# TensorE's program written out instead of looped, in a three-stage fp32 kernel (RWKV mixing, experts, output)

## The reference, cut to what matters

```python
xn = layernorm(x)                                   # x: (8, 512, 512) fp32
# attention branch (RWKV)
xk, xv, xr, xg = (xn + (prev(xn) - xn) * tm for tm in (tm_k, tm_v, tm_r, tm_g))
k, v, r, g = xk @ Wk.T, xv @ Wv.T, xr @ Wr.T, xg @ Wg.T          # 512 x 512 weights
wkv = scan over tokens: out = (a + e^u e^k v) / (b + e^u e^k); a, b = w a + e^k v, w b + e^k
attn = layernorm((sigmoid(r) * wkv * sigmoid(g)) @ Wo.T) * ln_g + ln_b
# expert branch, on z = rmsnorm(xn)
probs = softmax(z @ w_router); top 4 of 32 experts, at most 256 tokens each
out = sum over chosen e: weight * ((silu(z @ w_gate[e]) * (z @ w_up[e])) @ w_down[e])   # 512 x 352
out += sigmoid(z @ w_shared_gate) * ((silu(z @ sw_gate) * (z @ sw_up)) @ sw_down)       # 512 x 1408
result = x + attn + xn + out
```

## Time and profile before

| | |
|---|---|
| device time, median of 3 runs | 1700.39 us (1694.39 to 1702.78) |
| the profiled execution: span from the first to the last instruction | 1694.5 us |
| TensorE busy with matmuls | 1649.4 us, 97% of the span |
| VectorE busy | 1273.3 us, 75% |
| GpSimd busy | 840.5 us, 50% |
| ScalarE busy | 698.3 us, 41% |
| mean granted TensorE clock | 0.994 of full speed |

### The profile page before, as it was taken

How to read it: one execution, slowest core, us unless ns; L and a number is a source line. 1 busy time by engine, 2 the same in 40 slices (tenths; PEclk the granted TensorE clock), 3 DMA queues, 4 the chain that set the end, 5 groups by cost and what they waited for, 6 DMA issues and landing times.

```text
span 1694.5 us, 26244 instructions
## 1 busy us (share of the span) xinstructions
PE 1649.4 (97%) x8512; PEld 1404.6 (83%) x8512; DVE 1273.3 (75%) x1863; ACT 698.3 (41%) x1216; POOL 840.5 (50%) x691
## 2 busy tenths in 40 slices
PE   6989999999999999999998999999999999999999
PEld 5768887877999999999986888887788878888887
DVE  7988999998656565556589787776777767687776
ACT  5755655654666666666653221121121212112121
POOL 4587777775444444444467444352434425243351
PEclk9999999999999999999999999999999999999999
DMA  4534343425766666666686654554544343433431
GB/s 173 203 129 174 138 160 125 172 81 215 261 237 232 227 227 238 237 241 242 230 276 222 229 180 150 200 167 161 160 143 162 122 144 113 156 106 115 164 99 52
DMA packets 122427, 299.16 MB, mean 177 GB/s; under 512 B 19997, under 2 KB 31261, under 8 KB 117729
## 3 DMA queue, kind: packets, MB, share of 16 engines
q1 hardware_dynamic: 103104, 263.82, 43.8%
q0 software_dynamic: 18944, 33.66, 7.0%
q10 hardware_dynamic: 288, 0.52, 0.1%
HBM read 233.34 MB, written 81.35 MB: 186 GB/s over the span
## 4 chain that ended last, share of the span: by engine, by line
PE 76%; DVE 14%; issue 6%; ACT 2%; POOL 2%; DMA 0%; DVEq 0%; ACTq 0%; POOLq 0%; SPq 0%
PE bank L2176 26%; PE bank L1400 16%; PE bank L2190 13%; PE bank L1427 8%; PE bank L2207 5%; PE bank L1024 5%; DVE mixf L719 3%; PE bank L1392 2%; DVE bank L687 1%; DVE st L667 1%; DVE mix L726 1%; DVE zT_lo L694 1%; DVE s_wg L2027 1%; PE bank L958 1%; DVE sr L740 1%
## 5 line engine op out<-in xcount | busy, mean ns | idle before, releaser
L1024 PE MATMUL bank<-mix,w 128*128 128x512 f32 x1488 | 353.8, 395 | 9.7 <-DVE ekv L735 4.9
L1024 PEld LDWEIGHTS bank<-mix,w 128*128 128x128 f32 x1488 | 277.7, 189 | 72.6 <-DVE ekv L735 5.5
L2176 PE MATMUL bank<-s_zT,s_wu 128*128 128x512 f32 x1056 | 257.0, 393 | 7.6 <-DVE bank L1932 7.6
L2176 PE MATMUL bank<-s_zT,s_wg 128*128 128x512 f32 x1056 | 255.7, 391 | 7.1 <-issue 7.1
L2190 PE MATMUL bank<-s_wd,s_h 128*128 128x512 f32 x1056 | 253.9, 389 | 0.0
L2176 PEld LDWEIGHTS bank<-s_zT,s_wu 128*128 128x128 f32 x1056 | 199.8, 190 | 51.1 <-issue 9.3
L2176 PEld LDWEIGHTS bank<-s_zT,s_wg 128*128 128x128 f32 x1056 | 199.1, 189 | 49.4 <-issue 7.9
L2190 PEld LDWEIGHTS bank<-s_wd,s_h 128*128 128x128 f32 x1056 | 198.6, 188 | 41.4
L1210 POOL TENSOR_TENSOR e_wg<-e_g_in,e_wg 128x1408 fp32r<-128x1408 f32 x31 | 100.8, 3250 | 213.1 <-ACT e_wg L1234 213.1
L1707 POOL DMA_INDIRECT s_picked<-y_rows,s_slot x128 | 141.0, 1101 | 81.7 <-DVE s_total L1988 43.2
L1816 ACT ACTIVATE s_act_g<-bank 128x512 f32<-128x512 f32 x88 | 52.6, 597 | 305.7 <-PE bank L2176 302.4
(11 more groups left out here) (188 smaller groups left out, 2490.1 us busy)
## 6 DMA issues: line engine op xcount, KB each, us to landing
s_wu<-wu_split SPq DMA_DIRECT2D x77, 512.0 KB
e_g_in<-in_w_gate SPq DMA_DIRECT2D x32, 704.0 KB
e_u_in<-in_w_up SPq DMA_DIRECT2D x32, 704.0 KB
e_d_in<-in_w_down SPq DMA_DIRECT2D x32, 512.0 KB
y_rows<-e_y SPq DMA_DIRECT2D x32, 512.0 KB, 2.9
s_zT<-zT_parts SPq DMA_DIRECT2D x16, 1024.0 KB, 6.8
zT_parts<-zT_hi SPq DMA_DIRECT2D x8, 1024.0 KB
zT_parts<-zT_lo SPq DMA_DIRECT2D x8, 1024.0 KB
```

The lines of the kernel that those rows point to most:

```text
L1024: last = pe.matmul(pj[m][:], w[i][:, w_part, k, m * P:(m + 1) * P], mix[:, i % 2, k, x_part, :], start=(k == 0 and q == 0), stop=(k == KC ...
L2176: last = pe.matmul(into[:], w[:, w_part, k, :], zT[:, x_part, k, :], start=(q == 0 and k == 0), stop=(q == 2 and k == KC - 1))
```

## The change

TensorE's functions for the three stages no longer use the loops on the engine. Plain Python loops call the same `one_round` and `one_expert` with numbers in place of counters, so that all 8 rounds, 32 experts and 8 rounds stand in its program one after the other. The four other engines keep their loops. Nothing is computed differently, and no DMA transfer, buffer or semaphore changes.

```diff
@@ project_stage, tensor
-        rounds(pe, first_round, one_round, last_round)
+        first_round()
+        for b in range(1, LAST):
+            one_round(b, b % 2, b // 2, second=b == 1, tail=b == B - 2)
+        last_round()
@@ expert_stage, tensor
-        return lambda: turn(0, 0, 1), lambda: experts(pe, one_expert)
+        def run():
+            for e in range(E):
+                one_expert(e, e % 2, min(2, E - 1 - e), e // 2 + 1)
+
+        return lambda: turn(0, 0, 1), run
@@ output_stage, tensor, main
             gate_up(0, 0, 0, 0)
-            rounds(pe, one_round)
+            for b in range(B):
+                one_round(b, b % 2, b < B - 1, b // 2)
```

## The result

The changed kernel takes 1691.31 us (median of 11 runs, 1688.91 to 1693.99) where the kernel before took 1701.51 us (11 runs, 1694.39 to 1703.68). The ratio is 0.995, with a 95% interval of 0.9937 to 0.9963: 6 to 11 us faster. The profiled execution took 1690.97 us, its span is 1689.2 us: the device time is some 1.8 us longer than the span.

The account below looks back on a forecast made before the run. TensorE's matmuls were taken to bound the kernel, with avoidable stops only at the output stage's two back-edges. 3.6 + 3.0 = 6.6 us off the median 1700.39 gave 1693.8 us, range 1686 to 1700.5 us.

Parts of the forecast that it names:

- What bounds the kernel: Whole kernel: TensorE's matmuls bound looped and written-out rounds alike; only the output stage's two back-edges cost, 6.21 and 3.17 us.
- Project and expert stage 0: Expert stage's 13 back-edges and the project stage's one: removing them wins 0, since periods across them are not longer.
- First back-edge, 3.6 us: Output stage: TensorE's own stop of 6.21 us goes, but `down` then waits for VectorE's stop, so 3.6 us won.
- the new wait: Output stage, first back-edge: TensorE's `down` of piece 0 waits 2.53 us for VectorE's `hidden_lo`.
- the sign of being right: Output stage: `down` newly waiting for `hidden_lo` 1.5 to 3 us after the first back-edge would confirm the forecast.
- Second back-edge, 3.0 us: Output stage: TensorE's stop goes and VectorE is in time by 0.3 us, so 3.0 us won.
- The clock: TensorE's clock behind the new wait: no halving expected as the wait is shorter than 2.65 us, priced at 0.
- the bound of 1.7 us: Most that half clock behind the new wait could cost: 12 matmuls in 4.58 us against 2.88 us.
- Fetches that are new, 0: Written-out code: about 67 instruction packets for 50, fetched ahead in straight code, costing 0.
- Rival D: Expert stage: its program comes late and TensorE stops there, making the kernel slower, 1710 us; chance 0.08.
- The sum: Whole kernel: 3.6 + 3.0 = 6.6 us won, from the median 1700.39 to 1693.8 us, 0.4% less.
- rival A: Output stage: VectorE's stop shrinks or TensorE's median stops are longer; 9.4 us or more won, 1691.0 to 1687; chance 0.22.

Follow-up runs that it names:

- pad12: Kernel before with all its loops, plus 12 small transposes on TensorE in round 0 of the output stage; ratio 0.9955, 8.1 us faster.
- dve_out_only: Kernel before with VectorE's output stage written out, TensorE still looped; ratio 1.0003.
- half_exp_pad15: Kernel before with TensorE's experts 15 to 28 written out and 15 small transposes more in round 0 of the output stage; ratio 0.9994.
- pe_out_only: Kernel before with TensorE written out in the output stage alone, project and expert stages looped; ratio 0.9943, 9.6 us faster.
- proj_two_exp: Kernel before with TensorE's project stage and two experts written out, output stage looped; ratio 0.9985.

## Why the prediction was right, point by point

- *What bounds the kernel*: right. TensorE's rounds and experts take the same time to 0.01 us written out as looped (100.64 and 13.62 us), and the two project periods of the earlier trace rows are 49.18 and 49.43 us for 49.17 and 49.42, so register arithmetic, counters and branches cost nothing.
- *Project and expert stage 0*: right for the full change. The rule of the Trainium skill (Runtime: NRT & Kernel Launch, "Instruction fetch mechanics") that a taken branch outside a window of two 16 KiB pages waits for a fetch is not borne out as it stands: the project body of 981 instructions, 3.8 such pages, was fetched once and jumped back without a stop, the output body of 1855 was fetched anew. What the same skill says of the size (Advanced Engine Details and Errata, "ISA Cache": a line of 16 KB holds 256 instructions) agrees: with boundaries every 256 instructions, the stops moved as placed.
- *First back-edge, 3.6 us*: the mechanism was right, the size off. 5.1 us were won. The failed term is VectorE's stop, taken over from the kernel before at 6.36 us. It was 4.54 us after the change, and 4.31 to 6.82 us in the kernels above, and the new wait 0.77 us instead of 2.53, below the 1.5 to 3 us that were named as the sign of being right. What sets the length of VectorE's fetch was not settled; it does not need TensorE's to be long (6.82 us in pad12, where TensorE has no stop).
- *Second back-edge, 3.0 us*: right, 3.13 us by the periods.
- *The clock*: no half clock behind the new wait in the changed kernel, as taken, and the bound of 1.7 us was met in pad12 (4.58 us for 12 matmuls, after a wait of 2.80 us). But the reason given was wrong, and the outcome luck: the prediction took a wait shorter than 2.65 us to be safe because that stop had left the clock at 1.00. Other executions had the clock fall after shorter stops at the same back-edge (timelines of dve_out_only and half_exp_pad15, with granted clocks of 0.58 and 0.51 behind them), and in pe_out_only it stayed at 1.00 after a longer wait:

```profile
1394.34 3.54 PE L2177 MATMUL bank<-s_zT,s_wg 128*128 128x512 f32 x9 [2.46 <-issue]
1395.23 3.78 PE L2188 MATMUL bank<-s_zT,s_wg 128*128 128x512 f32 x9 [2.26 <-issue]
929.98 3.00 PE L2176 MATMUL bank<-s_zT,s_wu 128*128 128x512 f32 x12 [3.02 <-DVE bank L1932]
```
- *Fetches that are new, 0*: right. 67 packets as forecast, no stop in the expert stage. Rival D is out.
- *The sum*: 6.6 us forecast, 1693.8 us; 1691.31 measured, 10.2 us less than before. The output stage of the profiled executions gives 8.2. Two more profiled executions with both stops (dve_out_only, half_exp_pad15) have 10.07 and 11.58 us of excess in their two periods, against 9.38 in the one that the sum was made from, while those without TensorE's stops have 0 to 1.9, pad12's half clock apart. So the one execution was on the low side, as rival A allowed for. Part of that is the clock: behind the second stop the 9 matmuls took 3.54 and 3.78 us in those two, and 2.25 us in the kernel before as profiled. The prediction also compared unlike things when it set the span of 1694.5 us beside the device times: with the 1.8 us between them the profiled execution took about 1696.3 us, some 5 us less than the median of 1701.51. How the remaining 2 us divide, the profiles can't say. The sum came out 3.6 us short of what was won, and the forecast held because its range was wide enough for that.
- What the prediction did not see: that the stops depend on where the loop's body lies. It read them as the price of TensorE's loop. The loop body of the output stage was, with 8 instructions left, near the worst place; at 38 instructions or more nearly all of the gain is there without writing anything out.

## What to carry to other kernels

An idle time of TensorE with no releaser, always the same few instructions behind a loop's back-edge, is the next piece of its program; ask first how many instructions lie between the body's start and the next multiple of 256 (with the origin set by a stop that was seen), since moving the body by 24 instructions was worth nearly as much here as writing the loop out, and an unrelated edit upstream can win or lose the same 8 us. When one engine's jump is removed, look for the other engines' jumps at the same place: they stand beside it and set what can be won. And take the size of such a stop from several executions, since VectorE's went from 4.3 to 6.8 us at one place whose own program was unchanged.

## What the runs showed of the hardware

- TensorE's program came in packets of 16 KB (0.82 MB in 50), one per 256 instructions or so (17,378 instructions in 67 packets after the change). A loop body of 981 instructions stayed in its store over a back-edge (no such packet from 209 to 317 us), one of 1855 did not (50 packets where one pass is 31), wherever it lay (48 in pad12).
- After a taken branch into code that is not there, the piece after the one at the body's start came about 4.2 to 5.4 us (first back-edge) or 2.9 to 3.3 us (second) after the body had begun. More was moved around the first (234 GB/s from 1181 to 1193 us in the kernel before, 151 from 1389 to 1400), but that this is the reason was not tested. The jump itself showed as a stop of TensorE of at most 0.36 us; what covers the fetch of the first piece, work that TensorE still has in its queue perhaps, was not tested either.
- VectorE stopped for 3.4 to 6.8 us at each back-edge of the same loop, directly behind the jump. In the middle of the stage it has 2.85 us to spare against TensorE, so only the rest shows.
- The length of an idle time did not by itself decide what TensorE's granted clock did next. It fell to 0.50 after 2.77 us (kernel before), to 0.58 after 2.46 us (dve_out_only), to 0.51 after 2.26 us (half_exp_pad15) and after 2.62 us it was 0.66 over 12 matmuls that took 4.20 us (proj_two_exp). It stayed at 1.00 after 2.65 us (kernel before) and after 2.75 and 3.02 us (pe_out_only).
